# Three of four layer norms: deviations from TensorE by way of ScalarE, where VectorE subtracted a mean

## The reference, cut to what matters

```python
def _layernorm(x, axis=-1, eps=1e-05):
    m = jnp.mean(x, axis=axis, keepdims=True)
    v = jnp.var(x, axis=axis, keepdims=True)
    return (x - m) / jnp.sqrt(v + eps)

h = _layernorm(x) * (1 + ca) + sa           # norm 1
x = x + ga * _L0_attn_ref(h, ...)           # softmax attention, 16 heads
h = _layernorm(x) * (1 + cb) + sb           # norm 2
x = x + gb * _L0_ffn_ref(h, ...)            # 16 experts, the best 4 weighted
# second layer, new ca, sa, ga, cb, sb, gb
h = _layernorm(x) * (1 + ca) + sa           # norm 3
x = x + ga * _L1_attn_ref(h, ...)           # running sums over the tokens, rotated
h = _layernorm(x) * (1 + cb) + sb           # norm 4
x = x + gb * _L1_ffn_ref(h, ...)            # gated mix with the token before
```

## Time and profile before

| | |
|---|---|
| median of 3 runs | 1416.08 us (1415.26 to 1417.34) |
| profiled execution: its own time | 1416.36 us |
| its span, first to last instruction | 1414.6 us |
| PE busy | 1193.8 us, 84% |
| DVE busy | 1144.3 us, 81% |
| ACT busy | 974.0 us, 69% |
| POOL busy | 277.1 us, 20% |
| granted TensorE clock, mean | 0.985 |

### The profile page before, as it was taken

The page is one execution under the profiler, slowest core; times in us unless marked ns, Lnnn a source line. Parts: engine busy times, 40 slices in busy tenths (PEclk is TensorE's granted clock), DMA queues, the critical chain, the costliest instruction groups (busy, mean ns, idle before and its releaser), DMA issues.

```text
span 1414.6 us, 22143 instructions
## 1 busy us (share of the span) xinstructions
PE 1193.8 (84%) x6834; PEld 894.0 (63%) x6834; DVE 1144.3 (81%) x2122; ACT 974.0 (69%) x1717; POOL 277.1 (20%) x260
## 2 busy tenths in 40 slices
PE   3767898988989898888989888898988889898887
PEld 2445585756757575665757566575756667575765
DVE  7525979798797979879797988879798897979765
ACT  1446776867677786767778676777867677787841
POOL 2312130311213020221313022131302213130210
PEclk9979999999999999999999999999999999999998
DMA  5320020303012030301103030210303021030000
GB/s 122 93 29 10 11 25 10 34 9 32 10 14 19 8 33 8 33 8 18 17 7 33 8 33 8 21 16 4 33 8 33 8 23 18 5 29 5 1 5 4
DMA packets 54663, 29.94 MB, mean 21 GB/s; under 512 B 3741, under 2 KB 53610, under 8 KB 54634
## 3 DMA queue, kind: packets, MB, share of 16 engines
q1 hardware_dynamic: 52744, 28.87, 15.4%
q10 hardware_dynamic: 1890, 0.70, 0.5%
HBM read 8.20 MB, written 2.10 MB: 7 GB/s over the span
## 4 chain that ended last, share of the span: by engine, by line
PE 51%; DVE 17%; ACT 16%; issue 12%; DMA 2%; POOL 1%; ACTq 1%; SPq 0%; DVEq 0%; POOLq 0%
PE ring L713 15%; PE pa L727 7%; PE pb L813 6%; DVE smax L1724 6%; PE pa L647 4%; PE ring L634 4%; ACT prob L1203 2%; DVE prod L1829 2%; PE ring L700 2%; PE pb_k L743 2%; PE ring L611 2%; ACT L1301 1%; ACT frac L1304 1%; ACT sin_t L1301 1%; DVE prod L1824 1%
## 5 line engine op out<-in xcount | busy, mean ns | idle before, releaser
L713 PE MATMUL ring<-ht,wgu 128*128 128x256 f32 x1024 | 241.8, 385 | 0.6 <-ACT sc_all L1250 0.5
L418 POOL TENSOR_TENSOR gsc<-gsc,sc_all 128x512 f32<-128x512 f32 x128 | 168.2, 1319 | 372.4 <-ACT gsc L1262 372.4
L1856 DVE TENSOR_TENSOR_SCAN prod<-keep,prod 128x512 f32<-128x512 f32 x188 | 224.3, 1214 | 0.0
L713 PEld LDWEIGHTS ring<-ht,wgu 128*128 128x128 f32 x1024 | 193.5, 191 | 34.5 <-issue 5.4
L1724 DVE TENSOR_REDUCE smax<-ring 128x4 f32<-128x1024 f32 x128 | 153.1, 1219 | 17.4 <-PE ring L611 14.7
L1789 DVE SCALAR_TENSOR_TENSOR prob<-prob,gsc 128x512 f32<-128x512 f32 x128 | 87.0, 689 | 94.4 <-POOL gsc L418 90.9
L813 PE MATMUL pb<-prod,wo 128*128 128x256 f32 x544 | 129.3, 382 | 18.9 <-DVE prod L1870 18.9
L1203 ACT ACTIVATE prob<-ring 128x1024 f32<-128x1024 f32 x128 | 125.6, 1023 | 8.7 <-PE ring L634 7.1
L727 PE MATMUL pa<-prob,wdown 128*128 128x256 f32 x512 | 123.1, 383 | 3.7 <-DVE prob L1789 3.7
L813 PEld LDWEIGHTS pb<-prod,wo 128*128 128x128 f32 x544 | 102.3, 190 | 34.8 <-DVE prod L1870 21.8
L1257 ACT ACTIVATE gsc<-ring,gub_t 128x256 f32<-128x256 f32 x256 | 110.5, 501 | 17.7 <-PE ring L713 17.7
(11 more groups left out here) (270 smaller groups left out, 2355.4 us busy)
## 6 DMA issues: line engine op xcount, KB each, us to landing
q_rows<-qk_part SPq DMA_DIRECT2D x144, 64.0 KB
k_rows<-qk_part SPq DMA_DIRECT2D x135, 64.0 KB
x_in<-in_L_attn_x_dram SPq DMA_DIRECT2D x16, 128.0 KB, 2.2
sc_all<-_L_ffn_gate_up_proj_dram SPq DMA_DIRECT2D x1, 2048.0 KB, 12.0
out_dram<-xo SPq DMA_DIRECT2D x16, 128.0 KB, 1.8
prob<-in_L_wmod_dram SPq DMA_DIRECT2D x2, 384.0 KB, 4.9
k_rows<-qk_part ACTq DMA_DIRECT2D x9, 64.0 KB
wo<-in_L_attn_Wo_dram SPq DMA_DIRECT2D x1, 512.0 KB, 7.3
```

The source lines that it names most:

```text
L418: pool.tensor_tensor(gsc[:, n % NG, :], gsc[:, n % NG, :], sca, ALU.mult).then_inc(S["gsc"], 1)
L713: last = mm(ring[:, n % 2, g * 512 + j * L:g * 512 + (j + 1) * L], lhsT=wgu[:, 2 * n + j, g, :], rhs=ht[:, :], start=True, stop=True, skip ...
L1856: nc.vector.tensor_tensor_scan(prod[:, h, n - 1, :], keep[:, :], prod[:, h, n - 1, :], 0.0, ALU.mult, ALU.add).then_inc(S["cu" + str(n)], 1)
```

## The change

The first matmul of norms 2, 3 and 4 multiplies by `cent_w`, the identity less 1/128, so that the deviations themselves stand in PSUM. `centre` leaves VectorE. ScalarE's `square` gets two steps: a copy of the deviations from PSUM into `cent` or `centb` (semaphore `dev`), and, waiting for that copy, the square of the SBUF tile as before. The wait for the earlier reader of the tile moves from VectorE to ScalarE with it. VectorE's `scale` waits for `dev` too. Setup gets one VectorE instruction for `cent_w` (`ident` less 1/128), and `mean_w` shrinks to one column. The orders in `first` and `step` stay as they are but for the removed entries. In `last` the lists of TensorE, ScalarE and VectorE are written in another order.

```diff
-        mean_w = sb("mean_w", [P, P])
+        mean_w = sb("mean_w", [P, 1])
+        cent_w = sb("cent_w", [P, P])
...
-            def mean(b, n, src, src_sem, ps, free):
+            def centre(b, n, src, src_sem, ps, free):
...
-                mm(ps[:, 0:L], lhsT=mean_w[:, :], rhs=src, start=True, stop=True,
-                   skip_group_check=True).then_inc(S["mean" + n], 1)
+                mm(ps[:, 0:L], lhsT=cent_w[:, :], rhs=src, start=True, stop=True,
+                   skip_group_check=True).then_inc(S["cent" + n], 1)
...
-            def square(b, n, c, s):
+            def square(b, n, ps, c, s):
                 need(act, "cent" + n, b, 1)
+                other, same = {"2": ("h2", 0), "3": ("h4", 0), "4": ("h3", 1)}[n]
+                need(act, other, b, same)
+                af(c[:, :], ps[:, 0:L], ACT.Copy).then_inc(S["dev" + n], 1)
+                need(act, "dev" + n, b, 1)
                 af(s[:, :], c[:, :], ACT.Square).then_inc(S["sq" + n], 1)
...
+                dve.wait_ge(*upto("pool", "ident"))
+                ts(cent_w[:, :], ident[:, :], 1.0 / D, None, ALU.subtract)
...
-            def centre(b, n, src, dst, ps):
-                need(dve, "mean" + n, b, 1)
-                other, same = {"2": ("h2", 0), "3": ("h4", 0), "4": ("h3", 1)}[n]
-                need(dve, other, b, same)
-                tt(dst[:, :], src[:, :], ps[:, 0:L], ALU.subtract).then_inc(S["cent" + n], 1)
...
             def scale(b, n, c, ps):
                 need(dve, "rbc" + n, b, 1)
+                need(dve, "dev" + n, b, 1)
...
             def last(b):
+                phase_values(b, 0)
                 phases(b, 0)
-                phase_values(b, 0)
+                time_values(b, 0)
                 phases(b, 1)
```

More of the change, by code:

```diff
@@ L558, in variance @@
                 for t in range(NT):
-                    last = mm(ps[:, L + t:L + t + 1], lhsT=sqt[:, t * P:(t + 1) * P], rhs=mean_w[:, 0:1], start=True,
+                    last = mm(ps[:, L + t:L + t + 1], lhsT=sqt[:, t * P:(t + 1) * P], rhs=mean_w[:, :], start=True,
                               stop=True, skip_group_check=True)
@@ L1076, in last @@
             def last(b):
+                phase_values(b, 0)
                 phases(b, 0)
-                phase_values(b, 0)
+                time_values(b, 0)
                 phases(b, 1)
-                time_values(b, 0)
+                time_values(b, 1)
                 phase_values(b, 1)
-                time_values(b, 1)
+                sums_2(b, 0)
                 sums_1(b, 0)
-                sums_2(b, 0)
+                sums_2(b, 1)
                 sums_1(b, 1)
-                sums_2(b, 1)
+                phase_values(b, 2)
                 phases(b, 2)
+                time_values(b, 2)
                 memory_wo(b, 0)
-                phase_values(b, 2)
                 phases(b, 3)
-                time_values(b, 2)
                 memory_wo(b, 1)
@@ L1226, in second_norm_1 @@
             def second_norm_1(b):
-                square(b, "2", cent, sq)
+                square(b, "2", pa, cent, sq)
             def second_norm_2(b):
@@ L1278, in head_b @@
                 need(act, "xk", b, 0)
-                square(b, "3", centb, sqb)
+                square(b, "3", pb, centb, sqb)
                 need(act, "mod_b", b, 1)
@@ L1314, in fourth_norm_1 @@
                 need(act, "v3_ps", b, sums_done(b, CC))
-                square(b, "4", centb, sqb)
+                square(b, "4", pb, centb, sqb)
             def fourth_norm_2(b):
@@ L1440, in step @@
                 if on_a:
-                    square(a, "3", centb, sqb)
+                    square(a, "3", pb, centb, sqb)
                 if on_b:
@@ L1508, in first @@
                 clip_up(a, 7)
[L1509 removed]
+                square(a, "3", pb, centb, sqb)
                 modulate(a, "3", centb, hb[:, 1:L + 1], mod_b, 6)
             def last(b):
+                value(b, 0)
                 phase(b, 0)
[L1514 removed]
                 phase(b, 1)
```

58 lines of the change are left out of this document (21 added, 37 removed).

## The result

| | before | after |
|---|---|---|
| median | 1416.71 us of 4 runs (1415.26 to 1418.30) | 1432.44 us of 4 runs (1429.19 to 1434.92) |
| profiled execution | 1416.36 us, span 1414.6 | 1429.19 us, span 1427.5 |
| PE, DVE, ACT busy | 1193.8, 1144.3, 974.0 us | 1204.9, 1126.5, 992.7 us |
| granted clock, mean | 0.985 | 0.978 (0.958 to 0.979 in the four) |

The account below looks back on a forecast made before the run. No engine was taken as full; ScalarE's queue at norm 4 sets `x2`. Terms 3.5 - 0.42 - 0.2 + 0.2 = +3.1 us moved the median from 1416.08 to 1419.2 us, range 1415.8 to 1422.0.

Parts of the forecast that it names:

- a loop pass costs 0.41 - 0.16 = 0.25 us more: Loop: norm 4's cost less norm 3's gain, over fourteen steps, +3.5 us.
- Norm 4, +0.41: Norm 4 in the loop: the copy in ScalarE's full queue delays `up(a, 7)`, the scores and `x2` by 0.41 us.
- Norm 3, -0.16: Norm 3 in the loop: VectorE loses the subtraction, but `epsilon` waits for the variance, so 0.16 us is gained.
- Norm 2, 0: Norm 2 in the loop: copy and square just end before the variance's weights load, so 0 us.
- The step with a = 15, -0.42: Step without a next batch: norm 2's variance 0.67 us earlier, norm 4's 0.25 later, together -0.42 us.
- `last`, +0.2: New order in `last`: TensorE starts 0.26 us later, waiting for `xo`; with what follows, +0.2 us.
- The free norms, -0.2: Four norms in `first`, a = 15 and `last`: subtraction and hop become copy and hop, about -0.05 us each, -0.2.
- Setup, 0: Setup: the `cent_w` instruction stands where VectorE waits for the first scores anyway, so 0 us.
- B: Norm 2's square comes late, 0.1 us in each of 14 steps, 1.4 on top: 1420.6 us; chance 0.15.
- C: Norm 4's copy costs 0.31 us, norm 3 returns 0.25 or more: 1416.4 us, no change; chance 0.25.
- D: VectorE's queue is the limit, so each step gains the full 0.33 us: 1410.6 us, faster; chance 0.10.
- E: The copy could be free because it replaces something on ScalarE; no size or chance given.

Follow-up runs that it names:

- run 11: The kernel before with five unused matmuls per step in TensorE's two idle times, sized to fit them: 1416.01 us, ratio 0.9989.
- run 3: The changed kernel with norm 4 put back to VectorE's subtraction, norms 2 and 3 still converted: 1419.37 us, ratio 1.0016.
- run 10: The changed kernel with five unused matmuls per step in TensorE's two idle times, sized to fit them: 1422.60 us, ratio 1.0035.
- run 2: The changed kernel with norms 2 and 3 put back to VectorE's subtraction, only norm 4 converted: 1440.15 us, ratio 1.018.
- Run 14: The kernel before with `mean_w` 136 columns wide instead of 128, so the tiles behind it lie 32 bytes further: 1419.22 us, ratio 1.0017.
- run 15: The changed kernel with `mean_w` 16 columns wide (tiles 64 bytes further than in before) and five unused fitting matmuls per step: 1421.18 us, ratio 1.0025.

## Why the prediction was wrong, step by step

**The sum of the steps held; what it left out decided.** The prediction took the granted clock as 1.00 in every pass, because the pass of the earlier trace rows showed it. That is the step that failed: from "a loop pass costs 0.41 - 0.16 = 0.25 us more" to +3.5 us for fourteen steps. It is only true while TensorE's clock stays up, and 0.3 us in a pass were enough to change how often and for how long it fell: one fall of 1.6 us in before, three of 3.1 in after, 7.7 us more in the profiled pair. No rival named it, so the range couldn't hold the time either. The one pass of before that is 1.6 us longer than the others could have been read, and was not. The page's mean of 0.985 would have said little: of the 41.5 us that TensorE stood at 1.2 GHz in before, 3.4 lie in the loop, and run 11, with no fall in the loop, has 0.983.

- **Norm 4, +0.41: right in the sum, with some luck in its parts.** The copy and the square, then `up(a, 7)`, in a pass of after; the rows answer to the earlier trace rows:

```profile
947.54 0.44 ACT L1163 ACTIVATE centb<-pb 128x256 f32<-128x256 f32 x1
948.01 0.42 ACT L1165 ACTIVATE hb<-centb 128x256 f32<-128x256 f32 x1
948.33 0.82 ACT L1273 ACTIVATE prob<-ring,gub_t 128x256 f32<-128x256 f32 x2
```

  The copy costs 0.47 from start to start, not 0.41, and the square 0.32, but `up` takes 0.82 instead of 0.90, which the prediction didn't have, and the scores start 0.41 later, counted from the start of the pass, with the same wait of 0.21 for it; `x2` 0.40 later.
- **Norm 3, -0.16: right.** `epsilon` is 0.23 later at 0.40 later `x2`, so 0.17 came back, limited by the variance, as worked out.

```profile
955.72 0.53 PEld L560 LDWEIGHTS pb<-mean_w,hb 128*128 128x128 f32 x4
...
956.37 0.16 DVE L1674 TENSOR_SCALAR vepsb<-pb 128x2 f32<-128x2 f32 x1 [0.17 <-PE pb L560]
```

- **Norm 2, 0: right.** Copy and square end 0.05 later than the square before did, and the variance's weights load where they did.
- **The pass.** 0.25 inside a pass. At the turn of the loop TensorE's wait for the modulation is 0.80 or 1.04 us in after, in nearly alternate passes, and 0.90 in before; that makes 0.29 on the mean.
- **The step with a = 15, -0.42: right in kind, -0.28 in size.** Norm 2 gave -0.65 (forecast -0.67): its variance waits 0.92 in place of the 1.57 of the earlier trace rows. Norm 4 took back 0.41, not 0.25, since its variance, free of waits before, now waits for the square:

```profile
1320.56 0.61 PE L560 MATMUL pa<-mean_w,ht 128*128 128x1 f32 x4 [0.92 <-ACT ht L1165]
...
1358.37 0.61 PE L560 MATMUL pb<-mean_w,hb 128*128 128x1 f32 x4 [0.17 <-ACT hb L1165]
```

- **`last`, +0.2: right at a like clock (0.2 in runs 3 and 10), 0.9 in after.** The start was right in kind (the wait for `xo`), 0.36 later instead of 0.26. What varies from trace to trace is the clock again; in after it costs 0.6 behind the 32 products.

```profile
1370.71 2.05 PE L760 MATMUL pb_v<-hb,wv 128*128 128x256 f32 x4 [0.97 <-ACT xo L1337]
```

- **The free norms, -0.2: right as far as can be seen.** From the first scores to the first loop step traces with the same 30.7 us at 1.2 GHz behind the first 70 us of the span take 97.38 to 97.42 us where norms 2 and 3 have the old form (four traces and run 2) and 97.21 to 97.29 where they have the new one (six traces): 0.15 for two norms, forecast 0.1. The 0.6 us that after is later there has a lower clock behind it, 27.3 us at 1.2 GHz against 23.9 in before.
- **Setup, 0: wrong by 2 us on the median.** The instruction for `cent_w` costs nothing, as said (VectorE's later work starts within 0.3 us of before). What moved is where the tiles lie, which the diff shows in `mean_w`'s width and I didn't read as a change. Run 14 prices it at 2.1 us. The profiled execution of after happened to have only 0.05 of it.
- **Rivals.** B: no. C: no, norm 4 costs 0.41. D, faster: no. Run 3 shows what of it is true: at norms 2 and 3, where ScalarE idles, VectorE's relief gives 0.15 us a pass; at norm 4 it gives nothing. E: no.

With the clock up in the loop and the placement of before, the terms as measured are 3.5 - 0.3 + 0.2 - 0.15 = 3.25 us, which on run 11's 1416.0 makes about 1419.3, an estimate; the forecast was 1419.2. No run has just that. Runs 10 and 15 measured 1422.6 and 1421.2, with placements that cost up to 2.

**What stays open.** Why a fall lasts 3.4 us in passes of 81.5 to 81.8 and mostly 6.8 or more in those of 82.1 and up isn't shown; the runs show that it does. Nor is it shown why passes with the same waits fall or don't. Nor is it shown that the placement is the whole cause of the late first scores: one trace each, 39.1 and 40.2 us with the old placement, 40.6 to 41.8 with 64 bytes, 39.6 to 44.1 with 32. Which of the two idle times counts, or whether it takes both, wasn't tried.

## What to carry to other kernels

Before a change is priced by the row that ends a wait, read the granted clock pass by pass: if some passes of a loop are longer than their twins and the clock is under 1.00 in them, each edit that alters the length of a pass by a few tenths of a us is a draw in a lottery whose stakes (here 1.6 to 5 us a pass) are above the edit's own worth (0.25). Find TensorE's waits ahead of the fall and put matmuls there that fit inside them, measured against the wait (two, 1.13 us, in a wait of 1.21; not four, 1.99); only then compare two kernels. Compare other stretches at like clocks too: the order of `last` looked like 0.9 us and was 0.2. A tile's width that changes in a diff moves all tiles behind it, and that alone may be worth as much as the edit.
